# Gated cross-attention and block-sparse feed-forward on Trainium2: attention maxima as strided reductions, softmax steps on pairs of tiles

## The reference, cut to what matters

```python
kv = jnp.concatenate([context, latents], axis=1)
q, k = rms_norm(q, q_norm_w), rms_norm(k, k_norm_w)
scores = jnp.einsum('bhgqd,bhkd->bhgqk', qg, k) * scale
probs = jax.nn.softmax(scores.astype(jnp.float32), axis=-1)
out = jnp.einsum('bhgqk,bhkd->bhgqd', probs, v)
x = x + jnp.tanh(g_xattn[0]) * (out @ Wo)
```

## Time and profile before

| | us |
|---|---|
| median of 3 runs | 3668.18 |
| lowest and highest run | 3655.16, 3674.81 |
| span of the profiled execution | 3683.3 |

### The profile page before, as it was taken

The page is one execution under the profiler, slowest core; times in us unless marked ns, Lnnn a source line. Parts: engine busy times, 40 slices in busy tenths (PEclk is TensorE's granted clock), DMA queues, the critical chain, the costliest instruction groups (busy, mean ns, idle before and its releaser), DMA issues. The chain is left out here.

```text
span 3683.3 us, 52901 instructions
## 1 busy us (share of the span) xinstructions
PE 3184.8 (86%) x14138; PEld 2429.3 (66%) x14138; DVE 3152.2 (86%) x3890; ACT 2121.6 (58%) x3795; POOL 1668.6 (45%) x1175
## 2 busy tenths in 40 slices
PE   7978898889798988887989889878888888599699
PEld 5856666666476666665766666656666666277477
DVE  6856999999979999999799999988999999732666
ACT  3435666666656666666666666666666666431211
POOL 2322556555536555555455555544555555400000
PEclk9989999999999999999999999999999999799799
DMA  7870000000200000011000100110100000153400
GB/s 239 263 230 24 29 28 28 28 28 29 73 33 29 28 28 31 35 46 48 33 29 31 44 30 28 35 57 27 42 32 29 28 28 12 54 172 97 150 34 18
DMA packets 179314, 210.99 MB, mean 57 GB/s; under 512 B 10452, under 2 KB 125140, under 8 KB 174056
## 3 DMA queue, kind: packets, MB, share of 16 engines
q1 hardware_dynamic: 174408, 196.27, 16.2%
...
...
## 5 line engine op out<-in xcount | busy, mean ns | idle before, releaser
L855 POOL TENSOR_TENSOR att_sm<-att_sm,att_sc 128x512 f32<-128x512 f32 (+1 forms) x832 | 1305.6, 1569 | 545.9 <-ACT att_sc L732 490.1
L656 PE MATMUL att_ppv<-att_pr,att_V 128*128 128x512 f32 (+1 forms) x2880 | 907.6, 425 | 191.5 <-DVE att_pr L802 185.0
L732 ACT ACTIVATE att_sc<-att_sc 128x512 f32<-128x512 f32 (+1 forms) x960 | 611.9, 637 | 642.5 <-DVE att_sc L798 642.1
L802 DVE TENSOR_TENSOR att_pr<-att_sc,att_pr 128x512 fp32r<-128x512 f32 (+1 forms) x960 | 924.0, 964 | 0.7 <-ACT att_pr L736 0.7
L787 DVE TENSOR_TENSOR att_mx<-att_mx,att_sc 128x512 f32<-128x512 f32 (+1 forms) x832 | 883.6, 1062 | 41.2 <-ACT att_sc L729 38.5
L635 PE MATMUL att_pqk<-att_q,att_kT 128*128 128x512 f32 (+1 forms) x2880 | 881.3, 415 | 3.1 <-DVE att_kT L824 2.3
L605 PE MATMUL att_pkv<-att_ctxT,att_wkv 128*128 128x512 f32 (+1 forms) x3072 | 799.3, 384 | 75.9 <-DVE att_kT L824 71.8
L656 PEld LDWEIGHTS att_ppv<-att_pr,att_V 128*128 128x128 f32 (+1 forms) x2880 | 529.6, 198 | 421.4 <-DVE att_pr L802 318.0
L729 ACT ACTIVATE att_sc<-att_pqk,att_rk 128x512 f32<-128x512 f32 (+1 forms) x960 | 656.2, 684 | 129.1 <-PE att_pqk L635 123.8
L605 PEld LDWEIGHTS att_pkv<-att_ctxT,att_wkv 128*128 128x128 f32 x3072 | 564.0, 192 | 218.7 <-DVE att_kT L824 98.6
L736 ACT CAST att_pr<-att_sc 128x512 fp32r<-128x512 f32 (+1 forms) x960 | 599.3, 624 | 176.2 <-PE att_ppv L656 172.2
...
## 6 DMA issues: line engine op xcount, KB each, us to landing
q_scr<-pre_qT SPq DMA_DIRECT2D x128, 256.0 KB, 3.5
...
```

What stands on the lines that cost most here:

```text
L656: mm = pe.matmul(ppv[:], V[0:m, vp, t], pr[0:m, pp, (h * NT + t) % NP], start=(t == 0 and i == 0), stop=(t == NT - 1 and i == 2))
L732: act.activation(sc[0:m, s], sc[0:m, s], ACT.Exp).then_inc(exp_ok, 1)
L802: dve.tensor_tensor(pr[0:m, LO, s % NP], sc[0:m, s], pr[0:m, HI, s % NP].bitcast(F32), ALU.subtract).then_inc(plo_ok, 1)
L855: pool.tensor_tensor(sm[0:m, h], sm[0:m, h], sc[0:m, s], ALU.add).then_inc(sum_ok, 1)
```

## The change

- **Maxima.** Instead of a `tensor_tensor` maximum for each tile, a half has three `tensor_reduce` (groups `MAXG` of 6, 6 and 3 tiles). Their view of `sc` is turned, so that for each of the 512 columns the elements read one after another lie 512 fp32, or 2 KB, apart. The result of the first two goes to a free slot behind their tiles and is read with the next group (7 and 4 slots); `sc` has 17 slots a half, and the last tile's unused rows are set to a very low number once. So a half reads 17 x 512 elements a partition.
- **Pairs.** `exp`, `hi` and `lo` work on the pair that `sub` worked on before (groups `GR`: seven pairs and the last tile alone). `pr` has two slots of a pair. `sum` adds a pair as 128 x 1024 as soon as its exponentials are there, and one `fold` of 512 a half adds the two columns of the pair.
- **Order.** `LAG` is 24 instead of 21.5, with the value steps placed later; `vraw` keeps two chunks instead of all. The load of the head's split weights is two transfers, keys and values, each issued when its own half of the buffer is free.
- TensorE's steps are the same products on the same shapes.

The core of the diff:

```diff
-    NP = 3
+    NP = 2
     NR = NC + 1
-    assert NT % 2 == 1 and UT % NP == 0 and UT % 2 == 0 and HALF == 512 and NC == 4 and NT > 4 * (NC - 1) + 1 and CT <= NT
+    GR = [(t, min(t + 2, NT)) for t in range(0, NT, 2)]
+    NG = len(GR)
+    MAXG = ((0, 6), (6, 12), (12, NT))
+    SLOTS = NT + 2
+    MAXIMUM = 6
+    assert NT == 15 and NG % NP == 0 and UT % 2 == 0 and HALF == 512 and NC == 4 and CT <= MAXIMUM + 7
+
+    def slot(t):
+        return t + (t >= MAXG[1][0]) + (t >= MAXG[2][0])
...
-        vraw = sb("vraw", [P, NT * P])
+        vraw = sb("vraw", [P, 2, 512])
...
-        sc = sb("sc", [P, UT, HALF])
-        pr = sb("pr", [P, 2, NP, HALF], F32R)
-        mx = sb("mx", [P, NH, HALF])
-        sm = sb("sm", [P, NH, HALF])
+        sc = sb("sc", [P, NH, SLOTS, HALF])
+        pr = sb("pr", [P, 2, NP, 2, HALF], F32R)
+        sm = sb("sm", [P, 2, HALF])
...
-        LAG = 21.5
+        LAG = 24
...
-                steps += [(p, "qk", h, t), (p + 0.39, "copy", h, t)]
-                if t % 2 == 0:
-                    steps += [(p + LAG - 4.3, "sub", h, t)]
-                steps += [(p + LAG - 3.14, "exp", h, t), (p + LAG - 2.3, "hi", h, t),
-                          (p + LAG - 1.63, "lo", h, t), (p + LAG, "pv", h, t)]
-                if t >= 1:
-                    steps += [(p + 1.18, "max", h, t), (p + LAG - 1.5, "sum", h, t)]
+                steps += [(p, "qk", h, t), (p + 0.39, "copy", h, t), (p + LAG, "pv", h, t)]
+            for g, (t, z) in enumerate(GR):
+                p = h * NT + t + LAG
+                steps += [(p - 4.3, "sub", h, g), (p - 3.2, "exp", h, g), (p - 2.4, "hi", h, g), (p - 1.6, "lo", h, g)]
+                if g >= 1:
+                    steps += [(p - 1.9, "sum", h, g)]
+            for i, (t, z) in enumerate(MAXG):
+                steps += [(h * NT + z - 1 + 1.1, "max", h, i)]
             e = (h + 1) * NT
-            steps += [(e + 1.59, "mt", h, 0), (e + 1.47, "red", h, 0), (e + 3, "mb", h, 0)]
+            steps += [(e + 1.59, "mt", h, 0), (e + 1.7, "red", h, 0), (e + 3, "mb", h, 0)]
             f = e + LAG
-            steps += [(f - 0.6, "oraw", h, 0), (f + 0.67, "dt", h, 0), (f + 1.83, "dred", h, 0), (f + 3.76, "db", h, 0),
-                      (f + 4.21, "on", h, 0), (f + 4.31, "st", h, 0)]
+            steps += [(f - 0.6, "oraw", h, 0), (f - 0.5, "fold", h, 0), (f + 1.17, "dt", h, 0), (f + 1.83, "dred", h, 0),
+                      (f + 3.76, "db", h, 0), (f + 4.21, "on", h, 0), (f + 4.31, "st", h, 0)]
             steps += [(h * NT - NT + .1, "ldq", h, 0)]
-        for c, (k, v, vt) in enumerate(((-12.7, 1, 10.6), (-9, 4, 15.5), (-3.21, 6.63, 20.25), (-1.5, 11.35, 24.37))):
+        for c, (k, v, vt) in enumerate(((-12.7, 1, 12.6), (-9, 6, 16.6), (-3.21, 13, 20.6), (-1.5, 17.5, 24.6))):
...
-        steps += [(-17, "ldw", 0, 0)]
+        steps += [(-28, "ldwk", 0, 0), (-10.4, "ldwv", 0, 0)]
...
-        loads = [(12.89, "ldw", 0, 0), (12.89 + .1, "ldlat", 0, 0)]
-        loads += [(z - 1 + LAG - 1.5 + .1, "ldx", 0, i) for i, (a, z) in enumerate(XP)]
+        loads = [(2, "ldwk", 0, 0), (19.6, "ldwv", 0, 0), (19.7, "ldlat", 0, 0)]
+        loads += [(z - 1 + LAG - 0.5, "ldx", 0, i) for i, (a, z) in enumerate(XP)]
...
+        def grouped(n, h, g):
+
+            return tiles(n, h, GR[g][1] - 1)
+
+        def maxima(u, i):
+            return u * len(MAXG) + i + 1
...
+                for h in range(NH):
+                    dve.memset(sc[:, h, slot(NT - 1)], -3.0e38).then_inc(cst_ok, 1)
...
-                    if what == "ldw":
-                        k = head + dn
+                    if what in ("ldwk", "ldwv"):
+                        k, a = head + dn, int(what == "ldwv")
+                        sp.wait_ge((k_ps, v_ps)[a], AHEAD + NC * n)
+                        sp.dma_start(wkv[:, a].bitcast(F32).rearrange("p c t n -> p (c t n)"),
+                                     scr["kv"][bass.ds(k, 1), :, a].rearrange("o p c t n -> (o p) (c t n)")
+                                     ).then_inc((wk_in, wv_in)[a], 16)
+                    elif what == "ldlat":
...
-                        pe.wait_ge(max_ok, AHEAD + (NT - 1) * (u + 1))
+                        pe.wait_ge(max_ok, AHEAD + maxima(u, len(MAXG) - 1))
                         pe.wait_ge(on_ok, AHEAD + u - 1)
                         for c in range(4):
-                            mm = pe.transpose(pred[:, c * P:(c + 1) * P], mx[:, h, c * P:(c + 1) * P], ident[:])
+                            mm = pe.transpose(pred[:, c * P:(c + 1) * P], sc[:, h, MAXIMUM, c * P:(c + 1) * P], ident[:])
...
-                            mm = pe.matmul(ppv[:], V[0:m, vp, t], pr[0:m, pp, (h * NT + t) % NP],
+                            mm = pe.matmul(ppv[:], V[0:m, vp, t], pr[0:m, pp, (t // 2) % NP, t % 2],
...
-                        pe.wait_ge(sum_ok, AHEAD + NT * (u + 1))
+                        pe.wait_ge(fold_ok, AHEAD + u + 1)
...
-                        act.wait_ge(sum_ok, AHEAD + sums(n - 1, h, t))
+                        act.wait_ge(sum_ok, AHEAD + T + 1 - UT)
                         if h == 0 and t % 4 == 0:
                             act.wait_ge(rk_ok, AHEAD + rk_signals(n, t // 4))
-                        act.activation(sc[0:m, s], pqk[0:m, s % 2], ACT.Copy, scale=rk[0:m, t:t + 1]).then_inc(sc_ok, 1)
+                        act.activation(sc[0:m, h, slot(t)], pqk[0:m, s % 2], ACT.Copy, scale=rk[0:m, t:t + 1]).then_inc(sc_ok, 1)
                     elif what == "exp":
-                        act.wait_ge(sub_ok, AHEAD + T + 1)
-                        act.activation(sc[0:m, s], sc[0:m, s], ACT.Exp).then_inc(exp_ok, 1)
+                        a, z = GR[t]
+                        act.wait_ge(sub_ok, AHEAD + grouped(n, h, t))
+                        m, i = rows(a), slot(a)
+                        act.activation(sc[0:m, h, i:i + z - a], sc[0:m, h, i:i + z - a], ACT.Exp).then_inc(exp_ok, z - a)
                     elif what == "hi":
-                        act.wait_ge(exp_ok, AHEAD + T + 1)
-                        act.wait_ge(pv_ps, AHEAD + T - NP + 1)
-                        act.copy(pr[0:m, HI, s % NP], sc[0:m, s]).then_inc(phi_ok, 1)
+                        a, z = GR[t]
+                        act.wait_ge(exp_ok, AHEAD + grouped(n, h, t))
+                        act.wait_ge(pv_ps, AHEAD + (grouped(n, h, t - NP) if t >= NP else u * NT - NT + GR[t - NP][1]))
+                        m, i = rows(a), slot(a)
+                        act.copy(pr[0:m, HI, t % NP, 0:z - a], sc[0:m, h, i:i + z - a]).then_inc(phi_ok, z - a)
...
-                        act.wait_ge(vt_ps, AHEAD + NC * (n - 1) + t + 1)
-                        act.copy(vraw[:, a:z], pkv[:, BANK["v", t], 0:z - a]).then_inc(vraw_ok, 1)
+                        act.wait_ge(vt_ps, AHEAD + NC * n + t - 1)
+                        act.copy(vraw[:, t % 2, 0:z - a], pkv[:, BANK["v", t], 0:z - a]).then_inc(vraw_ok, 1)
...
-                        dve.wait_ge(sc_ok, AHEAD + T + 1)
-                        if t == 1:
-                            dve.wait_ge(mt_ps, AHEAD + u - 1)
-                            dve.tensor_tensor(mx[:, h], sc[:, s - 1], sc[:, s], ALU.max).then_inc(max_ok, 1)
-                        else:
-                            dve.wait_ge(max_ok, AHEAD + (NT - 1) * u + t - 1)
-                            dve.tensor_tensor(mx[0:m, h], mx[0:m, h], sc[0:m, s], ALU.max).then_inc(max_ok, 1)
+                        a, z = MAXG[t]
+                        i, k = slot(a) - (t > 0), slot(z - 1) + 1
+                        dve.wait_ge(sc_ok, AHEAD + tiles(n, h, z - 1))
+                        dve.wait_ge(max_ok, AHEAD + maxima(u, t) - 1)
+                        dve.tensor_reduce(sc[:, h, k if t < len(MAXG) - 1 else MAXIMUM], sc[:, h, i:k].rearrange("p t n -> p n t"),
+                                          AX.X, ALU.max).then_inc(max_ok, 1)
...
-                        w = min(2, NT - t)
-                        dve.tensor_tensor(sc[0:m, s:s + w], sc[0:m, s:s + w],
+                        a, z = GR[t]
+                        m, i, w = rows(a), slot(a), z - a
+                        dve.tensor_tensor(sc[0:m, h, i:i + w], sc[0:m, h, i:i + w],
...
-                        dve.wait_ge(phi_ok, AHEAD + T + 1)
-                        dve.tensor_tensor(pr[0:m, LO, s % NP], sc[0:m, s], pr[0:m, HI, s % NP].bitcast(F32),
-                                          ALU.subtract).then_inc(plo_ok, 1)
+                        a, z = GR[t]
+                        m, i, w = rows(a), slot(a), z - a
+                        dve.wait_ge(phi_ok, AHEAD + grouped(n, h, t))
+                        dve.tensor_tensor(pr[0:m, LO, t % NP, 0:w], sc[0:m, h, i:i + w], pr[0:m, HI, t % NP, 0:w].bitcast(F32),
+                                          ALU.subtract).then_inc(plo_ok, w)
...
-                        pool.wait_ge(exp_ok, AHEAD + T + 1)
+                        a, z = GR[t]
+                        m, i, w = rows(a), slot(a), z - a
```

(19 more changed lines are left out.)

31 lines of the change are left out of this document (13 added, 18 removed).

## The result

| | us, median (lowest to highest) |
|---|---|
| before, 4 runs | 3671.5 (3655.2 to 3684.9) |
| change, 4 runs | 4234.2 (4222.1 to 4261.4) |
| ratio, 95% interval | 1.154 (1.148 to 1.159) |

What follows compares the result with a forecast made beforehand. VectorE bounds attention, TensorE close behind. VectorE's 76 us plus 5.5 idle give rounds of 81.5 instead of 87.6: 195 us saved over 32 rounds, less 15 at ends, 3503 profiled, 3488 as median; range 3400 to 3910.

Steps and rivals of the forecast that it cites:

- The price of a strided element: VectorE's reductions for the maxima: 1.04 ns an element despite the 2 KB step, saving 8.7 us a round.
- Rival 1: VectorE's maxima: every strided element costs twice, 94.6 us a round, 3907 us; chance 0.25, 0.10 for a price between.
- threshold of 1.45 ns: VectorE's reductions: price an element from which VectorE's sum is back at 84 us a round.
- VectorE's sum: VectorE's work a round after the change: 76 us instead of 84.2, ends 64 and 86 at 1.04 ns an element.
- `lo` on pairs: VectorE's `lo` at 128x1024: 26% held up to 2.2 us by GpSimd's sums, 26.4 us a round, saved 0.4.
- the rule that one SBUF input isn't held: VectorE: only instructions with both inputs in SBUF stand still during GpSimd's sum, up to 1.10 us before the change.
- The broadcast `mb`: TensorE's queue: `mb` waits for the half before's subtractions, about 1.1 us twice a round, 2 us; ends 0 and 8.
- TensorE has the same products: TensorE's work a round: unchanged products, 70 to 71 us at full clock, 74 at the granted 0.95.
- Idle time: VectorE's idle time a round: 5.5 us instead of 3.4, as two equally long in-order queues wait for one another.
- rival 2: TensorE's waits for `lo` and `mb` eat the gain: 4 us more a round, 85.5, 3616 us; chance 0.15.
- `sub` no longer waiting for `pmax`: VectorE: the 1.8 us a round of this wait go, the first `sub` of a half standing 1.7 tiles behind `mb`.
- loads at no cost: Weight loads: two transfers instead of one cost nothing, with a free buffer half a round ahead and DMA 9% busy.

Runs made afterwards that it cites:

- b1_red: Kernel before with the strided reductions (and their 17 slots a half) alone, `red` moved to e + 1.7: 3896.2 us (1.059).
- e_after: The change with `mb` at e + 4 instead of e + 3 and the last chunk's value products at 14.7 instead of 17.5: 4117.4 us (1.119).
- a1_flat: The change with each reduction reading the same number of elements contiguously, so maxima of other elements: 3966.7 us (1.080).
- the probe: Kernel before plus 15 reductions of 2048 elements ahead of attention, steps of 1, 2, 3, 4 and 512 elements: 1.69 ns an element at 16 bytes.
- e_flat: The change with contiguous reductions (maxima of other elements), `mb` at e + 4 and the last chunk's value products at 14.7: 3638.9 us (0.990).
- b_stt: Kernel before with the running maximum taken from the scores in PSUM times the key's norm, only `mx` from SBUF: 3519.3 us (0.957).
- c_single: The change with `tensor_tensor` maxima and `exp`, `hi`, `lo`, `sum` on single tiles; its order, loads and slots stay: 4025.0 us (1.097).
- e_v: c_single with only the last chunk's value products moved, to 14.7 instead of 17.5: 4015.4 us (1.091).
- b_sum: Kernel before with only GpSimd's sums on pairs and one fold a half: 3716.8 us (1.013).
- e_single: c_single with `mb` at e + 4 instead of e + 3 and the last chunk's value products at 14.7 instead of 17.5: 3742.5 us (1.018).
- a2_tt: The change with the maxima of before, one `tensor_tensor` a tile; pairs and order stay: 4193.8 us (1.141).

## Why the prediction was wrong

**The price of a strided element: wrong, and enough by itself to turn the sign** (`b1_red` 1.059, `e_after` 1.119; the order is enough too, `a1_flat` 1.080). The step "I take 1.04, since each element is still one read of four bytes at the rate of the contiguous rows" failed; measured are 1.80 in the kernel and 1.69 in the probe. The rows offered nothing against it because every one of them reads at least two elements per 16 bytes. Rival 1 had the rule, and 0.35 went to it in all. Its threshold of 1.45 ns is 1.04 + (84 - 76) / 17.4 = 1.50 by its own numbers; no run has a price near it, so it isn't tested. At 1.80 its own sum is 76 + 13.1 - 1.1 + 2 = 90.0 a round, 3683 - 15 + 2.4 x 32 + 15 = 3760, so the order is needed beside it for 4234.

**VectorE's sum: right once the price is in.** 76 + 13.1 = 89 against 88.0 measured; in `e_flat`, at the assumed price, 75.5 against 76. (The upper end of 86 that stood beside it adds up to 85.) `lo` on pairs (26% held, 26.4 us) and the rule that one SBUF input isn't held both came out, for reductions, `sub` and, in `b_stt`, for a maximum.

**The broadcast `mb`: right mechanism, mis-sized.** I had 2 us a round, at most 8, from one VectorE chain of 4.7 against TensorE's 3.6. As a wait that is about right: 54.4 us at line 661 in the change, 1.7 a round, though 3.8 in `c_single` and 221.3 / 32 = 6.9 in `e_v`. As a cost it isn't. Moving `mb` gave (4015.4 - 3742.5) / 32 = 8.5 us a round on singles, with the `v` place right, and (4193.8 - 4010.2) / 32 = 5.7 on pairs, while the rows of the wait fell by 4.8 (221.3 to 66.6 us) and 2.0 (105.6 to 41.7). The rest is what comes behind the wait; late scores, late copies and an idle VectorE, which then is late for the next, are my reading of it. I priced a wait by its length and not by what it makes late. In the change no run moves `mb` alone; both places together gave 3.7 us a round.

**"TensorE has the same products": true, and it hid a wait.** I costed the value steps at new places at nothing. I never followed the bank that the last chunk needs to the step that frees it. That is the second fault of the order: 3.9 us a round in the waits of `c_single`, 1.4 in those of the change, and up to 175 us in all. The range, which took 8 us a round as its end for one wait, had no room for two.

**Idle time.** I took 5.5 us a round. It is 16 in the change and 10 in `e_flat` (85.7 us a round, 75.5 busy), so even with both faults of the order and the stride gone the change gains 1.0%, not 5%: 3638.9 us, near the 3616 of rival 2 and not my 3488. The row that rival 2 named, TensorE's wait for `lo`, is only 204 us there, 185 before. How these 10 split isn't settled: longer holds turned into waits, as in `b_sum`, may be part of it (pairs cost 92 us with both places repaired). Nor are the last 64 us of `e_single` taken apart; its two rounds of 87.0 and 90.5 us against 87.6 and the 15 us that I estimated for a longer `LAG` would make up most of them, and the 66.6 us in which TensorE still waits for `sub` lie in rounds like these.

**What came as forecast.** Reductions all alike and never held; `sub` no longer waiting for `pmax` (58.1 to 10.8 us); loads at no cost. TensorE waited for `sub` at line 661 32 times, not 64, and 1.7 us each time.

The 563 us in one chain, each link measured: order +353 (`c_single`), pairs +169 (`a2_tt`), reductions +40 (the change). In another chain, with the two places repaired: order +64, pairs +92, reductions +283 (with the wait for the bank that they bring), the two faults +117 (against 3679 beside those runs). The parts aren't additive, and each is large or small by what stands beside it: the two places are worth 117 to 359 us, the stride 267 to 479, the pairs 92 to 169.
